# Third graph layer: gathered rows put away to DRAM one turn sooner, the last four groups read in place, and the last three node blocks done in the same stage

## The chip, the cores and the metric

The kernel runs on one core of one Trainium2 chip. The metric is the device time of one execution in microseconds (us); less is better. The time before is 4120.34 us, the median of 3 runs (4119.45 to 4120.63).

## The reference, cut to what matters

Four graph layers run one after the other on the same graph of 6250 nodes and 106250 edges, 128 features a node. The change is in the third layer (`_L2_gnn_ref` of the reference):

```python
ei_all = x @ w_i
ej_all = x @ w_j
e = ei_all[idx_i] + ej_all[idx_j]
e = jnp.where(e > 0, e, 0.01 * e)
alpha = _segment_softmax(e, idx_j, n)          # softmax over the edges that share a source
msgs = alpha[:, None] * x[idx_j]
out = relu(jax.ops.segment_sum(msgs, idx_i, num_segments=n))
x = _layernorm(x + out)
# the fourth layer then needs, for every node and each of four relations r:
#   x @ weight[r] + bias[r]          (a table of 4 * 6272 rows, gathered per edge)
```

The softmax denominator belongs to the source node and the sum to the target node, so all edges have to be passed twice: once for the denominators, once for the weighted sums of gathered rows.

## The kernel before, in words

Edges are cut into tiles of 128; 8 tiles (`U`) make a group, 4 groups (`RING`) a turn. There are 104 groups (`GROUPS`) and 26 turns (`LAPS`). Nodes are in 49 blocks of 128 (`NB`). The program is a list of stages; at the end of each stage all engines meet at a barrier and the semaphores are cleared. A stage can be empty at run time: its engine programs stand in an `If` on a flag.

`layer2` (line 2732) is the third layer for this graph ("streamed"). It has two passes in one stage.

The first pass (lines 3109 to 3138 for VectorE, 2999 to 3027 for TensorE, `act_sums`, `sp_sums`) computes the scores and sums the denominators, group by group, in hardware loops. GpSimd isn't needed for it, so it already gathers node rows for the second pass (`gather_turns`, line 2929): for each group eight indirect DMAs of 128 rows into one of four slots of the buffer `G`. A full slot is put away to DRAM (`spill`, line 2786, to `SPILL`, in the profile `rows_ahead`), and the indices of the next group of that slot are copied to `IC` by ScalarE (`more_indices`, line 2791). GpSimd waits before a group for its indices and for `kept_rows`, the landing of the slot's last store. SyncE issues the stores, ScalarE copies the indices, each at fixed places of its own program: in the first pass, for slots 0 and 1 at group 1 of every odd turn, and for slots 2 and 3 at group 1 of the next even turn (lines 2825 to 2830, 2889 to 2894).

The second pass is unrolled in Python (`dve_turns`, `pe_turns`, `act_turns`, `sp_turns`). For each group SyncE loads the rows back from DRAM into a landing buffer (`sp_group`, line 2797), VectorE builds a weighted selection matrix `SEL` (128 x 8 x 96), TensorE multiplies rows and `SEL` (16 matmul records a group, line 2970), and VectorE adds the result to a window of `ACC` (line 676). There are two kinds of groups. The first `PICKED` = 56 were gathered from table `T2` before the denominators were known. For them the reciprocal denominator has to be picked out per edge: SyncE loads `LOD` (`source_in_block`), VectorE makes a one-hot matrix of it (`place_hot`, line 3039), TensorE multiplies (24 matmuls, line 2956), and VectorE does three more instructions (lines 3051, 3053, 3055) and one small one. Groups from `PICKED` on were gathered from table `T2C`, whose two extra columns hold that reciprocal (written at line 2864, just as the second pass begins); for them one small multiply (line 3059) does.

From turn 3 on each turn also finishes two node blocks (`copy_sums`, `mix_weighted`, `root`, `scales`, `write_rows`, `relations`, `keep_relations`, `store_rows3`), 23 chunks, 46 blocks. The last three blocks are done in a stage of their own, `rest2` (line 3206), which also loads the index list of the fourth layer.

In the second pass the remaining gathered groups (52 and on) are put away at places of an order written out by hand: `plan` (lines 2771 to 2780). It gives each pair of groups the first of the points (turn, 1) and (turn, 3) whose assumed time reaches 20.3 us for each pair. SyncE's program order there is: for (turn, b) load the rows of group (turn, b), load `LOD` for the next group, then the stores that the plan puts there, then at b = 1 the stores of the fourth layer's table. SyncE waits for the gather of a group before it issues its store, and all that stands behind waits too. ScalarE waits in the same way before it copies the next indices (`refill`, line 2896).

## Time and profile before

| | us |
|---|---|
| median of 3 runs | 4120.34 |
| profiled execution | 4121.19 |
| its span in the trace | 4119.4 |
| first pass of `layer2`, from the full ring on | 1835 to 2402 |
| second pass of `layer2` | 2402 to 2958 |
| `rest2`, to the first instruction of the next stage | 2958 to 2985 |

Times in the trace are us from the start of the span. DVE is VectorE, PE is TensorE, ACT is ScalarE, POOL is GpSimd, SP is SyncE; SPq is SyncE's issuing of DMAs. "<-" in brackets names what ended the idle time of the engine before the instruction. The add of line 676 runs once in each group, so its rows serve as marks: the mark of a turn is the one of its group 0.

### The profile page before, as it was taken

How to read it: one execution, taken by the hardware profiler on the slowest of the kernel's cores; microseconds unless marked ns; L12 is line 12 of the kernel's file. 1: busy time of each engine (PE TensorE's matmuls, PEld its weight loads, DVE VectorE, ACT ScalarE, POOL GpSimd, SP SyncE). 2: the span in 40 equal slices, each digit the busy share in tenths (PEclk: the TensorE clock that was granted, in tenths of full speed). 3: DMA queues.
4: the chain of work that ended last, by engine and by line, in shares of the span. 5: the costliest groups of instructions: out<-in, count | busy, mean ns of one | idle time of the engine just before them, and what ended most of it. 6: DMA issues, size and time to landing. Idle time of an engine off the chain costs nothing. (4 is left out here: it accounts for less than half of the span.)

```text
span 4119.4 us, 67476 instructions
## 1 busy us (share of the span) xinstructions
PE 2465.8 (60%) x18096; PEld 2169.4 (53%) x18096; DVE 2245.0 (54%) x6458; ACT 1038.2 (25%) x2890; POOL 2912.2 (71%) x3009
## 2 busy tenths in 40 slices
PE   2566666676647777529999977777633333333330
PEld 2454555454436666529999976666523333333330
DVE  5777777777744444436767668876522222222224
ACT  0244454444410111114444411111111111111112
POOL 2777777777747777626777777777377777777775
PEclk8555655656658898655555557767756556555655
DMA  4344444444425666446666678787545455444443
GB/s 121 97 113 129 116 132 128 117 130 115 130 71 144 146 147 147 80 95 176 183 182 176 185 217 262 249 246 250 178 122 130 129 134 132 129 132 132 130 129 94
DMA packets 454541, 602.65 MB, mean 146 GB/s; under 512 B 112602, under 2 KB 322350, under 8 KB 451086
## 3 DMA queue, kind: packets, MB, share of 16 engines
q1 hardware_dynamic: 344578, 392.09, 31.1%
q0 software_dynamic: 95744, 198.37, 22.2%
q10 hardware_dynamic: 14000, 9.82, 0.8%
q8 instruction: 69, 1.13, 0.1%
q14 instruction: 150, 1.23, 0.1%
HBM read 420.34 MB, written 184.16 MB: 147 GB/s over the span
## 5 line engine op out<-in xcount | busy, mean ns | idle before, releaser
L628 POOL DMA_INDIRECT G<-table,IC x2096 | 2002.2, 955 | 743.7 <-issue 633.3
L3342 DVE TENSOR_TENSOR_SCAN GW<-BIG,GW,PS 128x512 f32<-128x512 bf16 x208 | 266.2, 1280 | 781.6 <-PE PS L3317 766.8
L3317 PE MATMUL PS<-IDENT,G 128*128 128x128 f32 x832 | 204.2, 427 | 679.3 <-DMA G<-table,IC 679.3
L2936 POOL DMA_INDIRECT G<-table,IC x448 | 465.6, 1039 | 196.4 <-issue 139.0
L3317 PEld LDWEIGHTS PS<-IDENT,G 128*128 128x128 f32 x832 | 162.8, 223 | 717.7 <-DMA G<-table,IC 520.7
L2936 POOL DMA_INDIRECT G<-table2c,IC x384 | 369.8, 963 | 123.5 <-issue 116.2
L1284 PE MATMUL PS<-SEL,GW 128*128 128x96 f32 x1664 | 371.7, 414 | 78.1 <-DVEq L1360 78.1
L1284 PEld LDWEIGHTS PS<-SEL,GW 128*128 128x128 f32 x1664 | 347.2, 318 | 118.2 <-DVEq L1360 118.2
L2950 PE MATMUL PS<-BIG 128*128 128x49 f32 x1680 | 377.5, 412 | 1.1 <-ACT BIG L2885 1.1
L2950 PEld LDWEIGHTS PS<-BIG 128*128 128x128 f32 x1680 | 371.3, 333 | 1.3 <-ACT BIG L2885 1.3
L1162 ACT CAST BIG<-PS 128x490 bf16<-128x490 f32 x288 | 199.8, 706 | 257.1 <-PE PS L1149 252.4
L2970 PE MATMUL PS<-SEL,SCRATCH 128*128 128x96 f32 x1248 | 206.1, 334 | 94.0 <-DVE SEL L3062 93.9
L661 DVE TENSOR_TENSOR SEL<-PS,REL 128x768 f32<-128x768 f32 x262 | 249.1, 951 | 4.0 <-issue 0.2
L2970 PEld LDWEIGHTS PS<-SEL,SCRATCH 128*128 128x128 f32 x1248 | 191.8, 242 | 102.6 <-DVE SEL L3062 102.5
L2885 ACT ACTIVATE BIG<-PS,WE 128x128 f32<-128x128 f32 x832 | 226.4, 383 | 0.0
L1892 PE MATMUL PS<-SEL,G 128*128 128x96 f32 x864 | 142.0, 333 | 136.3 <-DMA G<-table,IC 136.2
L3265 ACT COPY IC<-BIG 128x8 int32 x104 | 20.5, 197 | 770.0 <-PE PS L3317 770.0
L1892 PEld LDWEIGHTS PS<-SEL,G 128*128 128x128 f32 x864 | 132.6, 242 | 143.5 <-DMA G<-table,IC 128.3
L1139 DVE TENSOR_SCALAR BIG<-BIG 128x245 bf16<-128x245 bf16 x624 | 190.9, 310 | 31.2 <-DVE SCRATCH L1365 29.3
L1149 PE MATMUL PS<-BIG 128*128 128x245 bf16 x624 | 159.9, 362 | 63.0 <-DVE BIG L1140 59.8
L3304 PE MATMUL PS<-IDENT,GW 128*128 128x128 f32 x840 | 195.6, 413 | 1.3 <-DVEq L3346 1.3
L3304 PEld LDWEIGHTS PS<-IDENT,GW 128*128 128x128 f32 x840 | 178.6, 228 | 1.5 <-DVEq L3346 1.5
(378 smaller groups left out, 4525.7 us busy)
## 6 DMA issues: line engine op xcount, KB each, us to landing
rows_ahead<-G SPq DMA_DIRECT2D x104, 520.0 KB
running_max<-BIG SPq DMA_DIRECT2D x105, 512.0 KB
GW<-source_in_block SPq DMA_DIRECT2D x160, 256.0 KB
G<-table,IC POOLq DMA_INDIRECT x2544
SCRATCH<-rows_ahead SPq DMA_DIRECT2D x78, 520.0 KB
SCRATCH<-edge_places SPq DMA_DIRECT2D x209, 192.0 KB
edge_counts<-BIG SPq DMA_DIRECT2D x24, 1568.0 KB
BIG<-run_mask SPq DMA_DIRECT2D x104, 256.0 KB
```

What stands on the lines that cost most here:

```text
L628: pool.indirect_dma_start(out=G[:, b, u, 0:width], out_offset=None, in_=table, in_offset=bass.IndirectOffsetOnAxis(ap=IC[:, b * U + u:b * ...
L661: return v.tensor_tensor(SEL[:, q], times(IOTAP, U), per(REL[:, ds(k, U)], W), ALU.is_equal)
L1162: a.copy(STAGE[:, s, :, at:at + nodes].rearrange("p h (w n) -> p w h n", w=2), PS[3 + 4 * q][:, 0:2 * SPAN].rearrange("p (w h n) -> p w h ...
L1284: t.matmul(PS[q][:, 0:W], GW[:, q, u, :], SEL[:, q, u, :], start=u == 0, stop=u == U - 1)
L1892: last = t.matmul(PS[q][:, 0:W], G[:, b, u, 0:D], SEL[:, q, u, :], start=u == 0, stop=u == U - 1)
L2885: ins = a.activation(PLACE[:, q, u, :], PS[3 + 2 * q + u // 4][:, (u % 4) * P:(u % 4 + 1) * P], ACT.Copy, scale=WE[:, q, u, 0:1])
L2936: pool.indirect_dma_start(out=GS[:, b, u, 0:width], out_offset=None, in_=table, in_offset=bass.IndirectOffsetOnAxis(ap=IC[:, b * U + u:b * ...
L2950: last = t.matmul(PS[0][:, 0:NB], PLACE[:, q, u, :], BLOCK[:, q, u, :], start=False, stop=False)
L2970: last = t.matmul(PS[q][:, 0:W], LANDED[b][:, u, 0:D], SEL[:, q, u, :], start=u == 0, stop=u == U - 1)
L3304: last = t.transpose(PS[4 + 2 * q + u // 4][:, (u % 4) * P:(u % 4 + 1) * P], RM[:, q, u * P:(u + 1) * P], IDENT[:])
L3317: last = t.transpose(PS[2 * q + u // 4][:, (u % 4) * P:(u % 4 + 1) * P], G[:, b, u, 0:D], IDENT[:])
L3342: v.tensor_tensor_scan(RM[:, q, h * 512:(h + 1) * 512], MB[:, q, h * 512:(h + 1) * 512], PS[2 * q + h][:], before, ALU.min, ALU.max).then_ ...
```

## The change

In the first pass all four slots are treated in one lap of two turns: slots 0 and 1 at group 1 of the even turn, 2 and 3 at group 1 of the odd turn, so each group is put away and its slot's next indices are copied one turn sooner; the loops need no special first lap and nothing behind them. `PICKED` goes from 56 to 60, so groups 56 to 59 are gathered from `T2` too and picked out. The plan starts with pair 26 at `PAIR * (pair - 26)` where it was `PAIR * (pair - 25)`, and the wait for the table's extra columns moves to pair 28. The last four groups (`KEEP` = 100 and on) aren't put away and loaded back: TensorE and VectorE read them in `G`. The three last node blocks and the load of the fourth layer's index list move from `rest2` to the end of `layer2`; `rest2` stays as a stage that is empty here.

```diff
-            PICKED = 56
-            column_in = sem("y_column")
+            PICKED = 60
+            KEEP = GROUPS - RING
+            column_in, idx_in = sem("y_column"), sem("y_idx")
...
-            for pair in range(26, GROUPS // 2):
+            for pair in range(26, KEEP // 2):
                 latest = (pair // 2, 1) if pair % 2 else (pair // 2 - 1, 3)
-                while points[place][0] < PAIR * (pair - 25) and points[place][1:] < latest:
+                while points[place][0] < PAIR * (pair - 26) and points[place][1:] < latest:
...
+            def rows_of(i, b):
+                return GS[:, b] if i >= KEEP else LANDED[b]
+
+            def rows_wait(eng, i, turn, b):
+                if i >= KEEP:
+                    eng.wait_ge(gathered[b], turn * (16 * U) + 16 * U)
+                else:
+                    eng.wait_ge(landed[b], turn * 16 + 16)
...
             def sp_group(sp, turn, b):
                 at = turn * RING + b
+                if at >= KEEP:
+                    return
...
-                            if b == 1 and h == 0 and keep0:
-                                spill(sp, lap * 4 - 2, 2, lap - 1)
-                                spill(sp, lap * 4 - 1, 3, lap - 1)
-                            if b == 1 and h == 1:
-                                spill(sp, lap * 4, 0, lap)
-                                spill(sp, lap * 4 + 1, 1, lap)
+                            if b == 1:
+                                for slot in (2 * h, 2 * h + 1):
+                                    spill(sp, lap * 4 + slot, slot, lap)
...
-                        sp_sums(sp, reg, 0, 1, False)
-                        sp_sums(sp, reg, 1, LAPS // 2, True)
-                        spill(sp, 50, 2, 12)
-                        spill(sp, 51, 3, 12)
+                        sp_sums(sp, reg)
...
                         store_rows3(sp, S, CHUNKS - 1, LEFT - 2, 2)
-                        sp.wait_ge(S.stored, 32 * CHUNKS + 32)
+                        sp.wait_ge(own_taken, PICKED)
+                        sp.dma_start(IDX3, IDX3D).then_inc(idx_in, 16)
+                        store_rows3(sp, S, CHUNKS, LEFT, NB - LEFT)
+                        sp.wait_ge(S.stored, 32 * CHUNKS + 32 + 16 * (NB - LEFT))
+                        sp.wait_ge(idx_in, 16)
...
-                                if b == 1 and h == 0 and fetch0:
-                                    more_indices(act, lap * 4 - 2, 2, lap - 1)
-                                    more_indices(act, lap * 4 - 1, 3, lap - 1)
-                                if b == 1 and h == 1:
-                                    more_indices(act, lap * 4, 0, lap)
-                                    more_indices(act, lap * 4 + 1, 1, lap)
+                                if b == 1:
+                                    for slot in (2 * h, 2 * h + 1):
+                                        more_indices(act, lap * 4 + slot, slot, lap)
...
                 def refill(act, turn, b):
                     for pair in plan.get((turn, b), ()):
-                        if pair == 26:
+                        if pair == (PICKED - RING) // 2:
                             act.wait_ge(column_in, 32)
...
                         act_turns(act)
+                        act.wait_ge(acc_chain, GROUPS + 2)
+                        copy_sums(act, S, CHUNKS, LEFT, NB - LEFT, False)
+                        root(act, S, CHUNKS + 1, NB - LEFT)
+                        write_rows(act, S, CHUNKS, LEFT, NB - LEFT, X, False)
+                        copy_turned(act, S, CHUNKS, NB - LEFT)
...
                         pe_turns(pe)
+                        turn_sums(pe, S, CHUNKS, NB - LEFT, False)
+                        turn_rows(pe, S, CHUNKS, NB - LEFT)
+                        relations(pe, S, CHUNKS, NB - LEFT)
...
-                        dve.wait_ge(acc_chain, GROUPS + 2)
+                        mix_weighted(dve, S, CHUNKS, LEFT, NB - LEFT)
+                        scales(dve, S, CHUNKS + 1, CHUNKS, NB - LEFT)
+                        keep_relations(dve, S, CHUNKS, LEFT, NB - LEFT)
+                        dve.wait_ge(S.kept, CHUNKS + 2)
...
 # rest2: each engine's program now stands in an If on the flag
-                    start_acts(act, S)
-                    copy_sums(act, S, 0, LEFT, nb, False)
...
+                    with act.If(is_general(act)):
+                        start_acts(act, S)
+                        copy_sums(act, S, 0, LEFT, nb, False)
...
```

With the new constants the plan (worked out from its few lines) puts the pairs at these points (turn, b), before and after: pair 26 (groups 52 and 53) at (0, 3) and (0, 1); 27 at (1, 3) and (0, 3); 28 at (2, 1) and (1, 3); 29 at (3, 1) and (2, 1); 30 at (4, 1) and (3, 1); 34 at (7, 1) and (6, 3); 39 at (11, 1) and (10, 3); 42 at (13, 3) and (13, 1); 43 (groups 86 and 87) at (15, 1) and (13, 3); 44 (88 and 89) at (16, 3) and (14, 3); 45 at (17, 3) and (15, 3); 49 at (23, 1) and (21, 1).

## Rows read from the trace of the kernel before

**Rows 1.** Stretches: busy us of PE, PEld, DVE, ACT, POOL; granted clock; DMA share; GB/s.

```profile
1835.00:2402.00 567.00, 566.28 (x5800) 566.12 (x5800) 395.46 (x1247) 267.61 (x1090) 410.98 (x392) 0.50 0.62 177
2402.00:2958.00 556.00, 403.98 (x3304) 356.99 (x3304) 420.16 (x879) 61.81 (x191) 394.20 (x410) 0.75 0.81 246
```

**Rows 2.** Waits in 2402:2958: waiter <- releaser: us in total, times, longest.

```profile
DVE GW L3039 <- DMA GW<-source_in_block: 28.1, 3, 14.6
...
PE PS L2970 <- DVE SEL L3062: 104.0, 65, 2.4
...
SPq L259 <- DMA G<-table2c,IC: 87.0, 18, 9.9
```

**Rows 3.** POOL in order of time: start, us, line, idle before and releaser.

```profile
1868.74 0.94 POOL L2936 DMA_INDIRECT G<-table,IC  x1 [33.52 <-ACT IC L2795]
...
2392.21 0.95 POOL L2936 DMA_INDIRECT G<-table,IC  x1 [0.30 <-issue]
...
2433.06 0.94 POOL L2936 DMA_INDIRECT G<-table,IC  x1 [0.30 <-issue]
2434.93 0.95 POOL L2936 DMA_INDIRECT G<-table2c,IC  x1 [0.93 <-DMA rows_ahead<-G]
...
2739.80 0.95 POOL L2936 DMA_INDIRECT G<-table2c,IC  x1 [0.30 <-issue]
...
2760.48 0.95 POOL L2936 DMA_INDIRECT G<-table2c,IC  x1 [0.30 <-issue]
```

**Rows 4.** DMA issues of SP in order of time: start, us until issued.

```profile
2408.97 0.38 SPq L2864 DMA_DIRECT2D table2c<-VC  x1
...
2416.85 0.35 SPq L2802 DMA_DIRECT2D PROD<-rows_ahead  x1
...
2429.04 0.84 SPq L2789 DMA_DIRECT2D rows_ahead<-G  x2
...
2571.22 8.32 SPq L2789 DMA_DIRECT2D rows_ahead<-G  x2
...
2743.02 0.34 SPq L2789 DMA_DIRECT2D rows_ahead<-G  x1
```

**Rows 5.** The column's DMA in 2405:2424: KB, us to landing.

```profile
table2c<-VC SPq DMA_DIRECT2D x1, 49.0 KB, 11.9
```

**Rows 6.** Marks of turns 4, 7, 14, 15 and 25 on DVE, and a stall.

```profile
2507.22 0.24 DVE L676 TENSOR_TENSOR BIG<-BIG,PS 128x96 f32 x1
...
2575.63 0.25 DVE L676 TENSOR_TENSOR BIG<-BIG,PS 128x96 f32 x1
...
2588.44 0.63 DVE L3039 TENSOR_SCALAR GW<-GW,PART 128x1024 bf16<-128x1024 bf16 x1 [5.66 <-DMA GW<-source_in_block]
...
2754.43 0.25 DVE L676 TENSOR_TENSOR BIG<-BIG,PS 128x96 f32 x1
...
2772.26 0.25 DVE L676 TENSOR_TENSOR BIG<-BIG,PS 128x96 f32 x1
...
2943.34 0.25 DVE L676 TENSOR_TENSOR BIG<-BIG,PS 128x96 f32 x1
```

**Rows 7.** All engines in order of time, from the last add on.

```profile
2957.57 0.94 SPq L1064 DMA_DIRECT2D table<-BIG  x2
2957.72 0.26 DVE L676 TENSOR_TENSOR BIG<-BIG,PS 128x96 f32 x1 [0.24 <-PE PS L2970]
...
2964.11 1.28 ACT L774 ACT_TABLE_LOAD   x1 [11.83 <-PEq L3436]
2965.41 0.51 ACT L774 COPY BIG<-BIG 128x384 f32<-128x384 f32 x1
...
2979.36 0.55 DVE L1019 TENSOR_TENSOR BIG<-PS,BIG 128x384 f32<-128x384 f32 x1
2980.01 1.53 SPq L1064 DMA_DIRECT2D table<-BIG  x3
2985.12 0.22 ACT L618 COPY IC<-BIG 128x32 int32<-128x32 int32 x1 [12.69 <-PEq L3436]
```

More of the change, by code:

```diff
@@ L2807, in sp_group, with sp_sums @@
                                  .to_broadcast([P, L])).then_inc(lo_in[1 - b % 2], 16)
-            def sp_sums(sp, reg, first, end, keep0):
-                with sp.Fori(first, end) as lap:
+            def sp_sums(sp, reg):
+                with sp.Fori(0, LAPS // 2) as lap:
                     for h in range(2):
@@ L2866, in _, with act_sums @@
                         store_rows3(sp, S, CHUNKS - 1, LEFT - 2, 2)
-                        sp.wait_ge(S.stored, 32 * CHUNKS + 32)
+                        sp.wait_ge(own_taken, PICKED)
[3 more added lines that the diff above has]
+                        sp.wait_ge(idx_in, 16)
                     sp.nop()
-                def act_sums(act, first, end, fetch0):
-                    with act.Fori(first, end) as lap:
+                def act_sums(act):
+                    with act.Fori(0, LAPS // 2) as lap:
                         for h in range(2):
@@ L2921, in _ @@
                         start_acts(act, S)
[L2922 to L2925 removed]
+                        act_sums(act)
                         act_turns(act)
+                        act.wait_ge(acc_chain, GROUPS + 2)
[3 more added lines that the diff above has]
+                        copy_turned(act, S, CHUNKS, NB - LEFT)
                     act.nop()
@@ L2966, in pe_group @@
                     pe.wait_ge(sel_ready, i + 1)
-                    pe.wait_ge(landed[b], turn * 16 + 16)
+                    rows_wait(pe, i, turn, b)
                     pe.wait_ge(added, i + 1)
                     for u in range(U):
-                        last = t.matmul(PS[q][:, 0:W], LANDED[b][:, u, 0:D], SEL[:, q, u, :],
+                        last = t.matmul(PS[q][:, 0:W], rows_of(i, b)[:, u, 0:D], SEL[:, q, u, :],
                                         start=u == 0, stop=u == U - 1)
@@ L3057, in dve_group @@
                     else:
-                        dve.wait_ge(landed[b], turn * 16 + 16)
-                        ce.step(v.tensor_tensor(WEP[:, q], NUM[:, ds(k8, U)], LANDED[b][:, :, D], ALU.mult))
+                        rows_wait(dve, i, turn, b)
+                        ce.step(v.tensor_tensor(WEP[:, q], NUM[:, ds(k8, U)], rows_of(i, b)[:, :, D], ALU.mult))
                     dve.wait_ge(pe_done, i + 3)
@@ L3212, in _ @@
                 def _(sp):
-                    sp.dma_start(IDX3, IDX3D).then_inc(idx_in, 16)
-                    sp.sem_inc(S.stored, 32)
-                    store_rows3(sp, S, 0, LEFT, nb)
-                    sp.wait_ge(S.stored, 32 + 16 * nb)
-                    sp.wait_ge(idx_in, 16)
+                    with sp.If(is_general(sp)):
+                        sp.dma_start(IDX3, IDX3D).then_inc(idx_in, 16)
+                        sp.sem_inc(S.stored, 32)
+                        store_rows3(sp, S, 0, LEFT, nb)
+                        sp.wait_ge(S.stored, 32 + 16 * nb)
+                        sp.wait_ge(idx_in, 16)
@@ L3219, in _ @@
+                    sp.nop()
                 @block.scalar
                 def _(act):
-                    start_acts(act, S)
-                    copy_sums(act, S, 0, LEFT, nb, False)
-                    root(act, S, 1, nb)
-                    write_rows(act, S, 0, LEFT, nb, X, False)
-                    copy_turned(act, S, 0, nb)
+                    with act.If(is_general(act)):
+                        start_acts(act, S)
+                        copy_sums(act, S, 0, LEFT, nb, False)
+                        root(act, S, 1, nb)
+                        write_rows(act, S, 0, LEFT, nb, X, False)
+                        copy_turned(act, S, 0, nb)
@@ L3227, in _ @@
+                    act.nop()
                 @block.tensor
                 def _(pe):
-                    start_pe(pe, S)
-                    turn_sums(pe, S, 0, nb, False)
-                    turn_rows(pe, S, 0, nb)
-                    relations(pe, S, 0, nb)
+                    with pe.If(is_general(pe)):
+                        start_pe(pe, S)
+                        turn_sums(pe, S, 0, nb, False)
+                        turn_rows(pe, S, 0, nb)
+                        relations(pe, S, 0, nb)
@@ L3234, in _ @@
+                    pe.nop()
                 @block.vector
                 def _(dve):
-                    start_dve(dve, S)
-                    dve.sem_inc(S.kept, 1)
-                    mix_weighted(dve, S, 0, LEFT, nb)
-                    scales(dve, S, 1, 0, nb)
-                    keep_relations(dve, S, 0, LEFT, nb)
+                    with dve.If(is_general(dve)):
+                        start_dve(dve, S)
+                        dve.sem_inc(S.kept, 1)
+                        mix_weighted(dve, S, 0, LEFT, nb)
+                        scales(dve, S, 1, 0, nb)
+                        keep_relations(dve, S, 0, LEFT, nb)
@@ L3244, in edges3 @@
+                    dve.nop()
         def edges3():
```

4 lines of the change are left out of this document (removed).

## The prediction

> **What bounds the kernel now.** I read the busy times of the stages first, then the waits of the second pass, and then its engines in order of time. In the first pass PE is busy for 566 of 567 us at half clock [rows 1]: nothing that POOL, SP or ACT do earlier there makes it shorter, so it stays as it is. POOL gathers beside it, waits once for 33.5 us (the first refill), and then runs without a gap: from 1868.74 to the last gather of group 51 at 2392.21 are 48 groups in 523.5 us, 21.8 us a pair, which is just the length of a turn (567 / 26) [rows 1, 3].
>
> The second pass is 556 us long. POOL's gathers in it end only 30 us before its end, so POOL looks like the bound. The waits say otherwise. DVE is busy for 420 us and PE for 404 [rows 1], and they wait for each other: PE 104 us for DVE's `SEL` [rows 2]. DVE's wait for a DMA is 28.1 us in 3 pieces: 14.6 as the pass begins, and two stalls of 5.7 and 7.8 [rows 2, 6], together 13.5. All three are for `source_in_block`, not for gathered rows. The two stalls come through SP: it waits 87 us for gathers, 18 times [rows 2], because the plan has it store a group that isn't there yet, and the load that DVE needs next stands behind that store. The row of two stores that took 8.32 us from 2571.22 ends 8.9 us before DVE gets its data at 2588.44 [rows 4, 6]. So the pass is the work of DVE and PE, with stalls wherever SP's place in the plan is more than some 5 us ahead of POOL. What decides is how far POOL is ahead of the plan, and the change moves both.
>
> **The plan's side.** Pairs 29 and 30 move a whole turn to the front, pair 34 and others half a turn; on average 20.3 us, one `PAIR`. If POOL isn't 20 us earlier too, SP waits longer than before.
>
> **POOL's side.** (a) Each group of the first pass starts a turn earlier: 21.8 us. Group 55 then ends at 2434.0 - 21.8 = 2412, and its indices are there, since each copy moves by a turn as well. (b) Group 56 needs the landing of group 52's store (`kept_rows`). Before, that store was issued at 2429.04 and POOL started group 56 at 2434.93, having waited 0.93 for it [rows 3, 4]. Now it is issued behind the second `source_in_block` load, where before the load of 2416.85 stood. But ahead of it in SP's queue is the write of the table's columns, issued at 2408.97, which takes 11.9 us to land, so to 2420.9 [rows 4, 5]; behind that two row loads of 520 KB and two of 256 KB, and then the store itself, 520 KB. At the 246 GB/s of the pass [rows 1] the whole 2.07 MB takes 8.4 us, the store alone 2.1. That bounds the landing by 2423.0 and 2429.3; I take 2427, toward the upper end, since little of the queue can move while the columns are being written. So POOL waits some 15 us at group 56 and starts it at 2427 instead of 2434.9: of the 21.8 us a lead of 7.9 is left (5.6 to 11.9). (c) From there on POOL runs at its own pace as before, so every later group is 7.9 us earlier: its lead over the plan shrinks by 20.3 - 7.9 = 12.4 us.
>
> **What DVE gets of it.** SP's waits grow by 12 us, and each one beyond its slack of some 5 us stalls DVE, until DVE is late enough; more stalls than the two of before, in turns 2 to 14. Their sum needs no guess, since the last binding point sets it. At (13, 3) SP now has to store groups 86 and 87. The last gather of group 87 ended at 2761.4, and a store follows the end of its last gather by 2.3 us (2743.02 against 2740.75) [rows 3, 4], so before 2763.7, now 2755.8. In the kernel before, the last store at that point (group 85) went out at 2743.02. From such a delayed store to DVE having its one-hot data took 8.9 us at a point with b = 1, of which some 1.7 is the table's store between; 7.2 gives 2763.0, and the add of the same group comes 4.5 us later (a picked group is 22.8 / 4 = 5.7 us, and the one-hot instruction stands about 1.2 into it). So the mark of turn 14 is at 2767.5, where it was at 2754.4 [rows 6]: 13.1 us late.
>
> **Four more picked groups.** Turn 14 becomes a picked turn. Picked turns took 22.8 us (2507.22 to 2575.63, three turns), or 23.6 over the seven turns to 2754.43 with the 13.5 of stalls taken off; turn 14 took 17.8 [rows 6]. That adds 5.0 to 5.8 us of DVE's and PE's own work, with nothing to hide it: I take 5.4. Behind it nothing binds: (14, 3) needs group 89, a pair of 20.3 us behind group 87, so at 2776.1; SP comes there just behind the mark of turn 14, at about 2769, 7 us early. At a point with b = 3 the slack is larger than with b = 1 by the table's store, and the next group, 60, needs no one-hot data any more, so I let it pass. Unpicked turns go at 17.1 us (ten turns from 2772.26 to 2943.34 [rows 6]), slower than POOL's pair rate asks for. Sum for the second pass: 13.1 + 5.4 = +18.5.
>
> **The last four groups in place.** Four stores and four loads go, 4.2 MB. In the last ten turns DVE has no wait for landed rows that I can find among its long waits [rows 2], turn 25 isn't slower than those before it, and the DMA share is 0.81 [rows 1]. So 0, between -2 and 0.
>
> **The last three blocks.** From the last add at 2957.72 to the next stage's first ACT instruction at 2985.12 are 27.4 us [rows 7]. The work itself, from ACT's copy at 2965.41 to the end of DVE's add at 2979.91, is a chain of 14.5 us and stays so. From the last table store to the next stage's ACT are 5.1 us with one stage boundary in it, and from the store at 2957.57 to ACT at 2964.11 6.5 us with two [rows 7]; an empty stage costs the difference of 1.4 at most. Afterwards: 0.3 + 14.5 + 5.1 + 2 x 1.4 = 22.7, so -4.7 (bounds: -7.5 if empty stages are free, -2 if the `If`s and instruction loading of the longer program cost as much as the boundary). The index list is loaded beside this chain in both.
>
> A place where the skill and the trace differ: ACT's table load before the copy at 2964.11 takes 1.28 us and the copy starts 0.02 us after it [rows 7], and this load goes with the change; it is inside the -4.7. The Trainium skill (ScalarE: Activation LUTs, "What ACT_TABLE_LOAD costs") counts a drain of 1.38 us beside the load's 1.283 for every switch. By the page the end would gain 1.4 us more; the row shows no drain here.
>
> **Sum.** Second pass +18.5, last groups 0, last blocks -4.7: +13.8. On the profiled execution's 4121.2 us that gives 4135.0; it stands 0.85 above the median of the runs, so 4134.2. About 0.2% (8 us) is what a measurement of this kernel tells from no change; this is +0.34%.
>
> **Rivals.**
> A, the forecast: POOL loses most of its lead at group 56, and SP's waits carry the rest to DVE. Own range: a lead of 11.9 gives +9.8, one of 5.6 +16.1; with 2 or 3 us for the other terms +7 to +19. 0.62.
> B, the lead stays: the store of group 52 lands by about 2414, or SP's slack is larger than I read. Then the plan and POOL move together by 20 us, SP's stalls are as before, and only the picked turn (+5.4) and the last blocks (-4.7) are left: +1, 4121. For it: the DMA engines had idle time before 2409. Against: the 11.9 us of the column write in the same queue [rows 5], and DVE's own 14.6 us wait behind it [rows 2]. 0.17.
> C, faster: the lead of 21.8 us stays and the pairs fall at points with more slack (34 and 39 move from b = 1 to b = 3, and both stalls of before were in turns 7 and 11), so that DVE's stalls vanish: -13.5, and the slower turns around them too, 7 x (23.6 - 22.8) = -5.6. With +5.4 and -4.7 that is -18, 4102; half of it 4111. It decides itself at the start of group 56: within 1 us of the end of group 55 it can be, with the wait of 15 us it can't. 0.09.
> D, worse: SP and POOL hold each other. A late store frees its slot late, POOL stops as at group 56, and the lead becomes negative, as SP's ten microseconds of waits become POOL's. With no lead left at all (group 56 at 2434.9) the shift is 7.9 more: +22, and with 4 us for slower turns (PE at half clock behind each stall) 4146. For it: SP would have waits of over 12 us in a queue that also carries the stores. Against: POOL waited for stores in the whole pass hardly at all. 0.12.
>
> **How the numbers follow.** The predicted time is A's, 4134. A's own range is 4127 to 4139. B and D belong to the 8 in 10, C and the ends of D don't: 4119 to 4144. Slower by over 0.2% (above 4128.6): most of A, all of D, 0.70. Within: B, a little of A and of C, 0.21. Faster (below 4112.1): C, 0.09.
>
> **What would show it.** POOL: first gather from `table2c` moves to group 60; before group 56 a wait of 13 to 17 us put down to `rows_ahead<-G`; then no gap. SP: waits for gathers above 87 us. DVE: more than two stalls at L3039 for `source_in_block`, the mark of turn 14 13 us later, turn 14 near 23 us, turns 15 to 25 at 17.1. End: from the last add to the next stage's first ACT instruction 22 to 24 us. The forecast is wrong if group 56 starts before 2420, or if DVE doesn't stall although SP waits.

## The result, and the profile after

The kernel with the change takes 4138.05 us (median of 5 runs, 4134.29 to 4143.79); the kernel before, run beside it, takes 4120.34 us (5 runs, 4117.63 to 4122.26). The ratio is 1.0044 [1.0031, 1.0057]: slower by 18 us, between 13 and 23. Here and below a ratio leaves out single executions far above the rest, of which there are two (4859 us in e6, 7544 us of the kernel before beside e13). The profiled span grows from 4119.4 to 4135.6 us, by 16.2. The forecast was 4134, with slower as the likeliest sign. The lines of the program have moved: the gathers are now at L2945 (before L2936), the stores at L2799, the row loads at L2814, the `LOD` load at L2818, `place_hot` at L3051, the write of the table's columns at L2870. Throughout, the mark of a turn is the add of its group 0, as in [rows 6].

The same two stretches as in [rows 1]: busy us of PE, PEld, DVE, ACT and POOL, granted clock, DMA share, GB/s.

```profile
1835.00:2402.00 567.00, 566.33 (x5800) 566.17 (x5800) 396.29 (x1248) 267.23 (x1089) 427.17 (x407) 0.50 0.63 179
2402.00:2958.00 556.00, 399.94 (x3326) 355.65 (x3326) 416.11 (x870) 60.65 (x187) 380.72 (x394) 0.73 0.78 238
```

The first pass is what it was: PE 566 of 567 us, and POOL does more beside it (427 against 411). In a window of the same length the second pass is now less busy on every engine: it waits more. The waits of 2402 to 2985 say on what (waiter, releaser, us in total, times, longest), against [rows 2]:

```profile
DVE GW L3051 <- DMA GW<-source_in_block: 44.8, 8, 14.5
...
PE PS L2979 <- DVE SEL L3074: 100.0, 64, 2.4
...
SPq L259 <- DMA G<-table2c,IC: 117.2, 21, 10.2
...
SPq L259 <- DMA G<-table,IC: 19.0, 3, 6.5
...
POOL G L2945 <- DMA rows_ahead<-G: 14.6, 3, 14.0
```

DVE's wait for its one-hot data grows from 28.1 to 44.8 us, SP's wait for gathers from 87.0 to 136.2 (117.2 and 19.0), and POOL has a wait of 14.0 us for a store, at the group where it had 0.93 [rows 3] (in the whole pass of the kernel before it waited 7.2 us for stores, in 8 pieces, the longest 4.5). POOL in order of time, start and duration first, the idle time before an instruction and its releaser in the bracket:

```profile
1847.74 0.94 POOL L2945 DMA_INDIRECT G<-table,IC  x1 [12.59 <-ACT IC L2805]
...
2428.35 0.94 POOL L2945 DMA_INDIRECT G<-table,IC  x1 [14.03 <-DMA rows_ahead<-G]
...
2469.43 0.94 POOL L2945 DMA_INDIRECT G<-table2c,IC  x1 [0.31 <-issue]
```

The first refill comes 21.0 us sooner (1847.74 against 1868.74), with a wait of 12.59 instead of 33.52. Group 56 starts at 2428.35 instead of 2434.93: of the 21 us of lead 6.6 are left. Group 60 is the first from `table2c`. SP's issues around it, start and us until issued:

```profile
2409.68 0.40 SPq L2870 DMA_DIRECT2D table2c<-VC  x1
2410.58 4.75 SPq L2814 DMA_DIRECT2D SCRATCH<-rows_ahead  x1
2415.44 0.37 SPq L2818 DMA_DIRECT2D GW<-source_in_block  x1
...
2416.86 4.33 SPq L2799 DMA_DIRECT2D rows_ahead<-G  x2
...
2463.89 7.31 SPq L2799 DMA_DIRECT2D rows_ahead<-G  x2
```

and what the DMA engines do in 2405:2424, in 40 equal slices of 0.475 us: busy tenths, GB/s, and below it the column write (KB, us from issue to landing), which took 11.9 us in [rows 5]:

```profile
DMA  4031050040508779999999999599659598997998
GB/s 138 0 95 43 0 138 0 17 121 0 138 1 14 13 14 107 52 11 6 4 7 4 49 47 27 35 87 95 52 78 157 96 201 271 271 191 164 216 279 359
...
table2c<-VC SPq DMA_DIRECT2D x1, 49.0 KB, 11.6
```

From the 16th to the 25th slice (2412.1 to 2416.9) the engines are busy at 9 tenths and more and move 31 GB/s on average, where the pass has 238. The row load issued behind the column write takes 4.75 us to issue, the two stores 4.33; in a quiet place two stores take 0.84 [rows 4]. So the first row loads and the stores of groups 52 and 53 alike are held up beside the column write. The kernel before has the same delay at its first row load (5.44 us to issue), but its store comes later. DVE's stalls and the marks (those of turns 14, 15, 25, and the last add), against [rows 6]:

```profile
2424.09 0.48 DVE L3051 TENSOR_SCALAR GW<-GW,PART 128x1024 bf16<-128x1024 bf16 x1 [14.54 <-DMA GW<-source_in_block]
...
2478.53 0.48 DVE L3051 TENSOR_SCALAR GW<-GW,PART 128x1024 bf16<-128x1024 bf16 x1 [7.82 <-DMA GW<-source_in_block]
...
2540.19 0.49 DVE L3051 TENSOR_SCALAR GW<-GW,PART 128x1024 bf16<-128x1024 bf16 x1 [6.19 <-DMA GW<-source_in_block]
...
2603.18 0.74 DVE L3051 TENSOR_SCALAR GW<-GW,PART 128x1024 bf16<-128x1024 bf16 x1 [6.40 <-DMA GW<-source_in_block]
...
2705.46 0.48 DVE L3051 TENSOR_SCALAR GW<-GW,PART 128x1024 bf16<-128x1024 bf16 x1 [8.51 <-DMA GW<-source_in_block]
...
2770.72 0.25 DVE L676 TENSOR_TENSOR BIG<-BIG,PS 128x96 f32 x1
...
2790.71 0.25 DVE L676 TENSOR_TENSOR BIG<-BIG,PS 128x96 f32 x1
...
2959.37 0.25 DVE L676 TENSOR_TENSOR BIG<-BIG,PS 128x96 f32 x1
...
2975.44 0.25 DVE L676 TENSOR_TENSOR BIG<-BIG,PS 128x96 f32 x1 [0.24 <-PE PS L2979]
```

Two long stalls (13.5 us) have become four (28.9). The 7.82 ends 7.3 us after the end of SP's two stores of 7.31 us, 2463.89 to 2471.20, just as the stall of before followed the stores of 8.32 us. The other two stand where the kernel before has its two: in turns 7 and 11, behind SP's stores at the points (7, 1) and (11, 1). For (11, 1) the rows are: in the kernel before the second store of the pair and the stall behind it, then the second store with the change, behind which comes the stall of 2705.46 above.

```profile
2681.09 0.34 SPq L2789 DMA_DIRECT2D rows_ahead<-G  x1
...
2691.48 0.68 DVE L3039 TENSOR_SCALAR GW<-GW,PART 128x1024 bf16<-128x1024 bf16 x1 [7.78 <-DMA GW<-source_in_block]
...
2695.83 0.34 SPq L2799 DMA_DIRECT2D rows_ahead<-G  x1
```

Worked out from the plan's lines, (11, 1) holds pair 39 before and pair 40 after, and (7, 1) pair 34 and pair 35: each point now asks for one pair more. One pair (20.3 us) less the lead of 6.6 is 13.7 us; the two stalls end 14.7 us (2603.18 against 2588.44) and 14.0 us later than before. DVE is late against the kernel before by 8.0 us at the mark of turn 3, by 14.3 at that of turn 5, and by 13.2 to 16.3 from there to turn 14: the two stalls that are new, in turns 2 and 4, make the delay, and the other two keep it.

The mark of turn 14 is 16.3 us later than before (2754.43), that of turn 15 18.4 (2772.26), that of turn 25 16.0 (2943.34), the last add 17.7 (2957.72 in [rows 7]). The end, all engines in order of time:

```profile
2975.72 0.51 ACT L774 COPY BIG<-BIG 128x384 f32<-128x384 f32 x1 [8.91 <-DVE BIG L676]
...
2989.51 0.55 DVE L1019 TENSOR_TENSOR BIG<-PS,BIG 128x384 f32<-128x384 f32 x1
2990.15 1.52 SPq L1064 DMA_DIRECT2D table<-BIG  x3
...
2999.59 1.28 ACT L618 ACT_TABLE_LOAD   x1 [17.21 <-PEq L3458]
3000.89 0.22 ACT L618 COPY IC<-BIG 128x32 int32<-128x32 int32 x1
```

From the last add to the next stage's ACT copy are 25.45 us (3000.89 - 2975.44), where [rows 7] have 27.40. The boundary ahead of the last blocks is gone, but the next stage now begins with a table load of 1.28 us, where it had none before.

The balance on the trace: second pass +17.7 (of it 0.6 from the start of the pass), end -1.95, sum +15.75 of the 16.2 by which the span grew.

### The profile page after: what moved, and what is told of

Its sections match the earlier page's. It is cut to its first block and busy times, and to the rows that moved or that the text cites. A ratio compares the mean times of both kernels' runs of the same rounds, so it can differ in the third digit from the quotient of the medians.

```text
span 4135.6 us, 67756 instructions
## 1 busy us (share of the span) xinstructions
PE 2471.2 (60%) x18192; PEld 2176.0 (53%) x18192; DVE 2252.4 (54%) x6474; ACT 1038.5 (25%) x2890; POOL 2913.0 (70%) x3009
## 3 DMA queue, kind: packets, MB, share of 16 engines
q0 software_dynamic: 95744, 198.34, 21.8%
## 5 line engine op out<-in xcount | busy, mean ns | idle before, releaser
L628 POOL DMA_INDIRECT G<-table,IC x2096 | 2000.5, 954 | 770.5 <-issue 631.7
L2945 POOL DMA_INDIRECT G<-table,IC x480 | 498.1, 1038 | 199.8 <-issue 148.1
L2945 POOL DMA_INDIRECT G<-table2c,IC x352 | 340.0, 966 | 107.3 <-issue 106.4
```

What stands on the lines that cost most here:

```text
L628: pool.indirect_dma_start(out=G[:, b, u, 0:width], out_offset=None, in_=table, in_offset=bass.IndirectOffsetOnAxis(ap=IC[:, b * U + u:b * ...
L2945: pool.indirect_dma_start(out=GS[:, b, u, 0:width], out_offset=None, in_=table, in_offset=bass.IndirectOffsetOnAxis(ap=IC[:, b * U + u:b * ...
```

## The experiments

There are twelve runs of eight kernels. Seven of them (e1 to e4, e7, e9, e10) were on two chips where every execution, the kernel before's too, takes some 5480 us. There POOL, DVE and SP wait much longer (POOL 562.6 us for copies of indices in e1, where the kernel before has 34.1 on a usual chip), and in e1 the second pass takes 834 us where it takes 530 on a usual one. Differences of this pass can't be explained from those, so four of the seven were run again on usual chips: e1 as e5, e2 as e6, e7 as e11, e9 as e12.

| run | us | kernel before | ratio, 95% | second pass: first mark to last add |
|---|---|---|---|---|
| before | 4120.34 | | | 529.9 |
| after | 4138.05 | 4120.34 | 1.0044 [1.0031, 1.0057] | 547.0 |
| e5, plan as before | 4118.30 | 4115.26 | 1.0011 [1.0002, 1.0020] | 533.3 |
| e6, early store | 4121.78 | 4115.26 | 1.0014 [1.0005, 1.0024] | 537.1 |
| e11, column on ACT | 4136.44 | 4118.07 | 1.0042 [1.0028, 1.0055] | 550.6 |
| e12, combined | 4110.71 | 4118.07 | 0.9984 [0.9975, 0.9993] | 519.0 |
| e13, combined, column later | 4106.35 | 4121.35 | 0.9963 [0.9952, 0.9975] | 522.9 |

### The plan's shift alone undone (e1, again as e5)

```diff
-                while points[place][0] < PAIR * (pair - 26) and points[place][1:] < latest:
+                while points[place][0] < PAIR * (pair - 25) and points[place][1:] < latest:
```

The assumed times of the points also depend on `PICKED`, so the plan is that of before up to pair 42 only; from pair 43 on (turn 14) it stays between half a turn and a whole turn ahead of it.

> The changed kernel with one constant back: the plan's times at PAIR * (pair - 25), so pair 26 stands at (0, 3) again. Theory A (SP reaches its stores ahead of the gathers, since the plan went 20 us to the front and POOL only 7): group 56 starts at about 2435, no lead at all, but SP's waits for gathers fall from 117 us back to about 87, DVE has 2 stalls behind source_in_block instead of 4, and the time falls by about 14 us, to 4122 to 4127. Rival B (the extra time is the work of four more picked groups and the end of the stage; the plan is only moved about): the time stays at 4135 to 4139. Rival C (a later group 56 costs what it is late): slower than the changed kernel by 7 us, 4145.

On the slow chip 1.0052 [1.0031, 1.0072] (5504.77 against 5477.48), which tells nothing apart. The same kernel on a usual one:

> The same kernel as e1_plan_as_before once more, since the chip of that run had DMAs that took several times longer (the kernel before took 5477 us there). With DMAs as in the profile of before, theory A: group 56 starts at about 2435, SP's waits for gathers back to about 87 us, 2 stalls of DVE behind source_in_block where the changed kernel has 4, 12 to 15 us less than the changed kernel: ratio to the kernel before 1.0005 to 1.0015. Rival B (four picked groups and the end are the cost, the plan doesn't matter): 1.0044 as the changed kernel.

Measured 1.0011 [1.0002, 1.0020]. The waits of the pass, and POOL at group 56:

```profile
DVE GW L3051 <- DMA GW<-source_in_block: 30.6, 5, 14.6
...
SPq L259 <- DMA G<-table2c,IC: 109.5, 23, 9.9
...
2432.42 0.94 POOL L2945 DMA_INDIRECT G<-table,IC  x1 [20.57 <-DMA rows_ahead<-G]
```

DVE has two long stalls again (6.0 and 8.7, at 2586.7 and 2689.0), and the pass is 13.7 us shorter than after's. SP's waits for gathers didn't fall to 87 us as expected: they are 111.4 (109.5 and 1.9 for the first table), so their sum alone doesn't tell how long DVE stalls. POOL's lead over the start of group 56 in the kernel before is smaller than in the kernel with the change (2.5 us against 6.6), and part of it is that this run's second pass begins sooner (column write issued at 2407.21 against 2408.97); so it isn't the lead by itself that costs or gives, but the lead less what the plan asks for. The ratio falls by 3.3 of the 4.4 thousandths: that is the plan's share. What is left is in the main the picked turn: turns 13 and 14 take 23.7 and 20.4 us against 20.2 and 17.8 of before, 6.0 together, of which the turns ahead of them give back 3.9.

### The stores of groups 52 and 53 ahead of the column write (e2, again as e6)

```diff
                             for group in (2 * pair, 2 * pair + 1):
-                                spill(sp, group, group % RING, group // RING)
+                                if pair > 26:
+                                    spill(sp, group, group % RING, group // RING)
...
+                        spill(sp, 52, 0, 13)
+                        spill(sp, 53, 1, 13)
                         sp.wait_ge(w_in, 48)
                         sp.wait_ge(settled, 1)
                         sp.wait_ge(column_in, 16)
                         sp.dma_start(T2C...[:, :, D:C], VC[:]).then_inc(column_in, 16)
```

> The changed kernel with the stores of groups 52 and 53 issued before the write of the table's columns instead of behind it; the plan stays. Theory A: POOL's wait of 14.0 us before group 56 goes, group 56 starts at about 2414, the lead of about 21 us matches the plan's 20 us, SP's waits for gathers and DVE's stalls are those of the kernel before (2 stalls, some 13 us), the mark of turn 14 comes 10 to 14 us sooner than in the changed kernel, and the time is 4122 to 4128. Rival B (four picked groups and the end are the cost): POOL starts sooner, the time stays at 4135 to 4139. Rival D (the stores now delay the column write and the first loads behind them): the first one-hot of the pass comes 3 to 5 us later and eats a third of the gain, 4128 to 4132.

Slow chip: 1.0040 [1.0022, 1.0057] (5501.97 against 5477.48).

> The same kernel as e2_early_store once more, for the same reason. Theory A: the wait of 14.0 us before group 56 is gone, group 56 starts at about 2414, the mark of turn 14 comes 10 to 14 us sooner than in the changed kernel, ratio to the kernel before 1.0005 to 1.002. Rival B: POOL starts sooner and the ratio stays at 1.0044. Rival D (the two stores hold up the column write and DVE's first data): 1.002 to 1.003.

Measured 1.0014 [1.0005, 1.0024]. DVE's and SP's waits of the pass, and all that POOL waited for stores:

```profile
DVE GW L3054 <- DMA GW<-source_in_block: 30.4, 3, 14.6
...
SPq L259 <- DMA G<-table2c,IC: 85.4, 16, 10.3
...
POOL G L2948 <- DMA rows_ahead<-G: 0.9, 3, 0.3
```

The wait at group 56 is gone, POOL keeps its whole lead (first gather from `table2c` at 2451.3 instead of 2469.4, of which 5.0 us are an earlier begin of the pass in this run), and with the plan still a `PAIR` forward SP's waits are those of the kernel before: 85.4 us against 87.0 [rows 2], two stalls of 7.1 and 8.6 us against 5.7 and 7.8. This is rival B made real: lead and plan move together. The mark of turn 14, counted from the first mark, comes 13.9 us sooner than after's (10 to 14 expected), and the pass is 9.8 us shorter. So e5 and e6 take one cause away from its two ends: the plan asks for 20 us of lead, and the wait for the store beside the column write leaves 6.6.

### The column write issued by ACT (e7, again as e11)

```diff
-                        sp.wait_ge(column_in, 16)
-                        sp.dma_start(T2C...[:, :, D:C], VC[:]).then_inc(column_in, 16)
...
                         act_sums(act)
+                        act.wait_ge(settled, 1)
+                        act.wait_ge(column_in, 16)
+                        act.dma_start(T2C...[:, :, D:C], VC[:]).then_inc(column_in, 16)
                         act_turns(act)
```

> The changed kernel with the write of the table's columns issued by ACT instead of SP, so that SP's first loads and the stores of groups 52 and 53 don't stand behind it. Theory A (it is the column write ahead in SP's queue that holds the store of group 52): POOL's wait before group 56 falls from 14.0 us to 3 to 8 (the store is issued at about 2413 and needs some 6 us to land), DVE's first wait falls from 14.6 us to 4 to 8, the lead of POOL grows by 6 to 10 us; second pass 10 to 16 us shorter than in the changed kernel, ratio to the kernel before 0.999 to 1.002. Rival E (the write occupies the DMA engines themselves, whatever queue it is in): both waits stay within 3 us of 14 and the ratio at 1.004.

Slow chip: 1.0060 [1.0047, 1.0073] (5523.25 against 5487.04).

> The same kernel as e7_column_on_act once more, since the chip of that run had the long DMAs (the kernel before took 5487 us there). With DMAs as in the profile of before, theory A: the wait before group 56 falls from 14.0 us to 3 to 8, DVE's first wait from 14.6 to 4 to 8, ratio to the kernel before 0.999 to 1.002. Rival E (the write occupies the DMA engines whatever its queue): both waits within 3 us of 14, ratio 1.004.

Measured 1.0042 [1.0028, 1.0055]. POOL at group 56, DVE's first wait, and of 2405:2424 the DMA queues (packets, MB, share of 16 engines), their 40 slices and the column's landing:

```profile
2424.25 0.94 POOL L2946 DMA_INDIRECT G<-table,IC  x1 [12.43 <-DMA rows_ahead<-G]
...
2418.38 0.49 DVE L3052 TENSOR_SCALAR GW<-GW,PART 128x1024 bf16<-128x1024 bf16 x1 [11.33 <-DMA GW<-source_in_block]
...
DMA  5021053777999978893477548999999999999999
GB/s 138 0 78 60 0 138 6 13 13 13 130 79 88 70 88 105 97 97 63 106 143 198 192 144 157 285 259 267 337 393 379 397 411 390 404 413 386 395 377 376
...
q1 hardware_dynamic: 1005, 3.15, 52.9%
q10 hardware_dynamic: 5409, 0.04, 15.0%
...
table2c<-VC ACTq DMA_DIRECT2D x1, 49.0 KB, 24.0
```

The step of the prediction that the store stands behind the column write in SP's queue fails as far as the queue goes. With the column in a queue of its own (q10) SP's issues are quick (no row load takes over 0.7 us), but the transfers aren't at first: from the 11th to the 20th slice (2409.8 to 2414.5) they move 92 GB/s, and only from the 21st to the 40th (to 2424) 315. The column's landing is put off from 11.6 to 24.0 us, to 2431, and POOL still waits 12.4 us. The column write and the 3 MB around it run side by side on the same engines, whoever issues them. The Trainium skill has this rule (DMA: Bandwidth & Descriptors, "Issuing engines are not separate DMA queues": the DMAs of SP, ACT and GpSimd run on the same 16 engines and interleave, and spreading them over engines saves issue time alone); this run agrees. How much of the 12.4 us is the column and how much the sheer 3 MB (at the 238 GB/s of the pass some 13 us) it doesn't tell: in 2405:2424 the column's packets take 15.0% of the engines' time, and SP's (q1) 52.9%.

### Parts alone, on the slow chips only (e3, e4, e10)

`PICKED` alone set back to 56 in the kernel with the change (e3):

```diff
-            PICKED = 60
+            PICKED = 56
```

The edit also moves points of the plan, pairs 44 to 49 by half a turn or a whole one, since their assumed times depend on `PICKED`.

> The changed kernel with PICKED = 56 instead of 60, all else as changed (groups 56 to 59 read the reciprocal from the table's columns again). Theory A: POOL's wait before group 56 stays at about 14 us and the stalls of turns 2 to 11 stay, since SP still waits; turn 14 is an unpicked turn again: -5 us at turn 15, perhaps 1 or 2 more or less where the last stores fall, so 4131 to 4135. Rival B (four picked groups are most of the extra 17.7 us): 4122 to 4127.

The last three blocks alone put into `layer2` of the kernel before (e4; the edit is that part of the change's diff):

> The kernel before with one part of the change alone: the last three node blocks and the index list's load at the end of layer2, rest2 empty. From the last add to the first gather of the next stage it took 28.4 us before and 26.5 in the changed kernel. Theory A: -1 to -3 us against the kernel before, 4117 to 4119.5, within what 5 rounds can just tell. Rival (the merge is worth the whole stage start that it removes, as I forecast): -4.7, 4115.6.

The last four groups alone read in place in the kernel before (e10; the edit is the `KEEP` part of the diff):

> The kernel before with one part of the change alone: the last four groups read in place in G, without stores and loads. In the changed kernel the stretch from the mark of turn 25 to the last add is 16.1 us, 1.7 more than before. Theory G (TensorE and VectorE reading G at the end costs nothing; the 1.7 us is the granted clock or the order of the last turn): between -1 and +1 us against the kernel before. Rival (reading G or waiting for the gathers costs DVE): +1.5 to +2 us, in turn 25.

Measured 1.0055 [1.0033, 1.0077], 0.9996 [0.9982, 1.0010] and 0.9995 [0.9984, 1.0006]. The last two say that neither part costs anything that can be measured, with the reserve that transfers are slower there; the first says nothing of a usual chip. None of the three was run again, so what these parts alone are worth on a usual chip stays open, but for what the traces of the other kernels show. One thing e4's trace does tell: with that part as its only edit the table load at the start of the last blocks is gone, and one of 1.28 us stands at the start of the next stage, as in the kernel with the change.

### What follows, put together (e9, again as e12)

```diff
-            PICKED = 60
+            PICKED = 56
...
-                while points[place][0] < PAIR * (pair - 26) and points[place][1:] < latest:
+                while points[place][0] < PAIR * (pair - 25.4) and points[place][1:] < latest:
                     place += 1
-                plan.setdefault(points[place][1:], []).append(pair)
+                plan.setdefault({26: (0, 1), 27: (0, 3), 28: (1, 3)}.get(pair, points[place][1:]), []).append(pair)
...
                             for group in (2 * pair, 2 * pair + 1):
-                                spill(sp, group, group % RING, group // RING)
+                                if pair > 26:
+                                    spill(sp, group, group % RING, group // RING)
...
+                        spill(sp, 52, 0, 13)
+                        spill(sp, 53, 1, 13)
                         sp.wait_ge(w_in, 48)
```

> The changed kernel with the stores of groups 52 and 53 ahead of the column write, PICKED = 56, and a plan in which only pairs 26 to 28 stand at the early points (0, 1), (0, 3), (1, 3) and the others at PAIR * (pair - 25.4), 8 us nearer to POOL than in the kernel before. Theory A: group 56 starts at about 2421 (its indices wait for the column), a lead of 12 to 14 us over a plan that moved by 8: SP's waits for gathers fall below 70 us, at most one stall of DVE behind source_in_block above 5 us is left after the first, no fourth picked turn: 6 to 12 us less than the kernel before, ratio 0.997 to 0.9985. Rival B (the plan doesn't matter): 0.999 to 1.0. Rival F (the stalls only move and keep their sum, since the plan's points are coarse against the slack): 0.999 to 1.0005.

Slow chip: 1.0029 [1.0017, 1.0041] (5500.29 against 5487.04).

> The same kernel as e9_all_56 once more, for the same reason. Theory A: group 56 starts at about 2421, SP's waits for gathers below 70 us, at most one stall of DVE above 5 us after the first wait, ratio to the kernel before 0.997 to 0.9985. Rival F (the stalls only move and keep their sum): 0.999 to 1.0005.

Measured 0.9984 [0.9975, 0.9993]: 4110.71 against 4118.07, faster by 0.7 to 2.5 thousandths. POOL at group 56, now from `table2c`, and the waits of DVE and SP in the pass:

```profile
2421.39 0.94 POOL L2948 DMA_INDIRECT G<-table2c,IC  x1 [7.73 <-ACT IC L2805]
...
DVE GW L3054 <- DMA GW<-source_in_block: 14.6, 1, 14.6
...
SPq L259 <- DMA G<-table2c,IC: 47.3, 10, 8.0
```

Of DVE's 28.1 us of waits for `source_in_block` [rows 2] only the first, 14.6, is left; the stalls that SP's place in the plan made are all gone. The run tells what the parts are worth together, not each. Group 56 again waits for the columns, but starts 13.5 us sooner than before.

### The first row loads ahead of the column write (e13)

To the kernel of e12:

```diff
-                while points[place][0] < PAIR * (pair - 25.4) and points[place][1:] < latest:
+                while points[place][0] < PAIR * (pair - 24.4) and points[place][1:] < latest:
...
-                        sp_group(sp, turn, b)
+                        if turn or b > 1:
+                            sp_group(sp, turn, b)
...
                         sp.wait_ge(column_in, 16)
+                        sp_group(sp, 0, 0)
+                        sp_group(sp, 0, 1)
                         sp.dma_start(T2C...[:, :, D:C], VC[:]).then_inc(column_in, 16)
```

> e12_all_56 with the loads of the first two groups (rows and source_in_block) issued ahead of the write of the table's columns, and the plan at PAIR * (pair - 24.4), 20 us later, since DVE starts earlier and POOL doesn't. If the column write occupies the DMA engines for its 12 us whatever stands around it (rival E, which e11 bore out), then what matters is what DVE has to do during it: DVE's first wait falls from 14.6 us to 4 to 7, a second wait of 2 to 6 appears at group 2, and the write lands 3 to 4 us later, so group 56 starts at about 2425 instead of 2421. Net 5 to 9 us less than e12_all_56, ratio to the kernel before 0.996 to 0.9975, if the later plan keeps the stalls away. If the loads ahead only delay the write and DVE waits as long at group 2 as it did at group 0: 0.998 to 0.999.

Measured 0.9963 [0.9952, 0.9975]: 15 us faster than the kernel before (4106.35 against 4121.35), the fastest of all. DVE's waits, its first two in order of time, SP's waits, and POOL at group 56:

```profile
DVE GW L3057 <- DMA GW<-source_in_block: 19.3, 5, 6.9
...
2415.30 0.49 DVE L3057 TENSOR_SCALAR GW<-GW,PART 128x1024 bf16<-128x1024 bf16 x1 [6.89 <-DMA GW<-source_in_block]
...
2428.47 0.49 DVE L3057 TENSOR_SCALAR GW<-GW,PART 128x1024 bf16<-128x1024 bf16 x1 [4.01 <-DMA GW<-source_in_block]
...
SPq L259 <- DMA G<-table2c,IC: 64.9, 12, 8.2
...
2427.36 0.94 POOL L2951 DMA_INDIRECT G<-table2c,IC  x1 [14.17 <-ACT IC L2805]
```

The first wait falls from 14.6 to 6.9 us and the first mark comes at 2419.7 instead of 2427.9. Half of it is paid back: a wait of 4.0 at group 2, and in all five waits of 19.3 us, more than e12's one of 14.6. The pass from the first mark on is 3.9 us longer than e12's, the last add 4.3 us sooner (2942.6 against 2946.9). In the trace that is a gain of 4.3 us over e12, and the medians differ by 4.4 (the ratios, each against its own runs of the kernel before, by 2.1 thousandths, 8.7 us, where 5 to 9 were expected). POOL pays with a start of group 56 that is 6 us later (4 expected), since the columns land later, which the plan (-24.4) was given room for. The earlier loads and the later plan were not run apart.

## Why the prediction was right, point by point

**First pass unchanged, POOL a turn sooner there.** Right: the refill 21.0 us sooner (forecast 21.8), group 55 ended 14.0 us before 2428.35, at 2414.3, with 2412 forecast.

**Group 56 waits for the store of group 52.** Right in size: 14.03 us with 15 forecast, start 2428.35 with 2427, lead 6.6 with 7.9. Half right in mechanism. The step said that the store stands in SP's queue behind the column write. Putting the store ahead of it removed the wait (e6); taking the column out of the queue left 12.4 of 14.0 us (e11). So the place in the queue makes little of the wait: the store has to run beside the column write and 3 MB of other transfers, and the split between these two stays open.

**The rest carried to DVE by SP.** Right, and this is the cause of the slowdown: e5 (plan back) and e6 (lead back) each remove some 70 to 75 per cent of it. SP's waits for gathers grew from 87 to 136 us, two stalls became four. Up to the mark of turn 13 DVE lost 13.7 us (2747.89 against 2754.43 less turn 13's 20.2), 13.1 without the 0.6 of the start. The forecast took 13.1 at the mark of turn 14, from a binding point at (13, 3), and that point didn't bind: SP did wait there, 6.7 us for its two stores,

```profile
2751.20 6.72 SPq L2799 DMA_DIRECT2D rows_ahead<-G  x2
```

but DVE has no stall behind it. The points that bind are (7, 1) and (11, 1), each with one pair more than before, and there the forecast's own difference, a pair less the lead, gives 13.7. So the rule behind the number was right and its place wrong; that (13, 3) gave the same 13.1 is partly luck, and that the stalls of the earlier turns already make the whole delay by the mark of turn 5 was not forecast. The long stalls alone would give 28.9 less 13.5, which is 15.4, of which turns 0 to 12 show 13.1.

**Four more picked groups.** Forecast 5.4, all in turn 14. Measured 2.6 in turn 13 (22.8 against 20.2: group 56 is prepared before the mark of turn 14) and 2.2 in turn 14 (20.0 against 17.8), 4.8 together; 6.0 in e5. That a part falls into turn 13 was overlooked; it is why turn 14 isn't near 23 us and its mark comes 16.3 us late instead of 13. Mark of turn 15: +18.5 forecast, +18.4 measured, 0.6 of it from the start.

**The turns behind.** Forecast 17.1 each, no change; measured 16.9 (168.7 over ten), 2.4 us less in all, and then 1.7 more from the mark of turn 25 to the last add (16.1 against 14.4). The 1.7 isn't the reading in place: e13 reads in place too and takes 14.5 from its mark to its last add. From turn 15 on the kernel before has odd turns of 16.3 us and even ones of 17.8, and the kernel with the change from turn 18 on the reverse, so that turn 25 falls on a long one. Turn 24 and what follows to the last add are 32.5 us together before and 32.4 after: the 1.7 goes with this alternation and isn't a loss. What makes the turns alternate stays open. Together with the 0 forecast for the reading in place the error is under 1 us.

**The last three blocks.** The weakest term: -4.7 forecast, -1.95 measured (-1.2 in e5, e6 and e11, -1.8 in e12, -1.9 in e13), just outside its bounds (-7.5 to -2); the end takes 25.45 us where 22 to 24 were the sign. The work between stayed (13.8 from ACT's copy at 2975.72 to DVE's last add at 2989.51, 13.9 in [rows 7]). Two things were mis-sized. The table load of 1.28 us was counted as gone with the separate stage, but another stands at the start of the next stage, in every kernel with the last blocks in `layer2`, e4 too; what places it there no run shows. The separate stage had a second load as well, in the shadow of DVE's work:

```profile
2965.94 1.28 ACT L822 ACT_TABLE_LOAD   x1
```

And an empty stage costs more than the 1.4 us read from the difference of two gaps: from the last store's issue at 2990.15 to the table load at 2999.59 are 9.4 us, where the same gap was 5.1 (2980.01 to 2985.12) in [rows 7], so two more boundaries cost 4.3, 2.15 each (9.2 to 9.4 us in e5, e6, e11, e12 and e13). Load and boundaries together are 1.28 + 2 x 0.75 = 2.8 us, the whole of the miss. The Trainium skill's drain of 1.38 us beside a table load (ScalarE: Activation LUTs, "What ACT_TABLE_LOAD costs") again has no gap in the rows: the load of 1.28 ends at 3000.87 and the copy starts at 3000.89. A drain ahead of that load would be hidden, since ACT stood idle, but the load of 2965.94 shows none there either: the copy before it ended at 2965.92.

**The sum.** +13.8 forecast and 15.75 on the trace: pass 17.7 instead of 18.5, end -1.95 instead of -4.7. That is 2 us of the 4 by which the measured median lies above the forecast; the profiled execution was itself 0.6 us under its median (4137.45 against 4138.05), where that of the kernel before was 0.85 over its own, which makes up most of the rest.

**The rivals.** B is what e6 made, +5.8 us instead of the +1 given to it; the end (3.5 less gained than thought in that run) and stalls 2.3 us longer account for that and 1 us more. C, a gain from stalls vanishing altogether, exists, but not in this change: e12 has it, with the stores ahead of the column write, another plan and the picked groups put back. D (POOL's lead going negative) didn't come: POOL's waits for stores are 14.6 us in all, 14.0 of it once.

## What to carry to other kernels

When a producer is started earlier and a hand-written order is moved forward by the same time, look for the one transfer that both need at the seam: the lead is worth only what is left behind it, and what the order asks for beyond that comes back, once the slack is used up, as stalls in whatever stands behind the waiting issue. A small transfer of thousands of pieces had to be moved in time to help here (behind the two stores in e6, behind the first loads in e13); another queue (e11) didn't help. A stage that is emptied but kept, and a table load that comes up again in the next stage, still have to be paid.

## What the runs showed of the hardware

- A write of 49 KB in pieces of 8 bytes (6272 of them) took 11.2 to 12.1 us from SP's queue with the loads behind it, 14.7 behind two row loads (e13), and 24.0 from ACT's queue beside SP's transfers (e11). For 4.8 us of it in SP's queue the engines showed as busy at 31 GB/s.
- Issued from ACT (e11) it took 15.0% of the engines' time in 2405:2424 (5409 packets). The other transfers went on beside it, at 92 GB/s up to 2414.5 and at 315 from there to 2424; the time of the kernel stayed the same (1.0042 against 1.0044).
- Chips differ by more than their clock: the same kernel took 4120 us on most and 5480 us on two (granted clock 0.63 and 0.60), with long waits for transfers and for what stands behind them, though a transfer of 3125 KB at the program's start landed after 9.7 us on either. Why is open. What holds for the stalls of one needn't hold for the other: e12's kernel is 0.9984 on one and 1.0029 (as e9) on the other.
- An empty stage costs about 2.1 us at run time (9.4 us between the last issue and the next stage's first ACT instruction, against 5.1 with two boundaries fewer).
- An ACT table load took 1.28 us, and the instructions on either side of it stood 0.02 us away (2965.92, 2965.94; 3000.87, 3000.89).
